# Softmax attentions: the values products of every step stand ahead of the step's other bank 7 work on TensorE

## Chip, cores and metric

The kernel is one program on one core of a Trainium2 chip. The metric is the device time of that core for one execution, in microseconds (us). Five engines work side by side, each through its own instructions in the order in which they are written: TensorE (PE; its weight loads are listed as PEld), ScalarE (ACT), VectorE (DVE), GpSimd (POOL) and SyncE (SP, here the issuer of most DMAs). They wait for one another by semaphores.

## What is computed

A chain of four layers, each an attention and a feed-forward part, each added to its input `x` after a layer norm. The rows are 4096 tokens of 128 features. Two of the attentions are softmax attentions with 16 heads of 8 features, and they alone are touched:

```python
# x: (16, 256, 128)
# L1_attn: causal, with biases
qkv = x @ Wqkv + bqkv
scores = einsum('bthd,bshd->bhts', q, k * D ** -0.5) + causal_mask
context = einsum('bhts,bshd->bthd', softmax(scores), v)
out = context.reshape(B, S, E) @ Wout + bout
# L3_attn, gated_attention: no mask, no bias
attn = softmax(einsum('bhqd,bhkd->bhqk', q, k) * HD ** -0.5)
out = moveaxis(einsum('bhqk,bhkd->bhqd', attn, v), 1, 2).reshape(b, l, d)
return out @ Wout * sigmoid(x @ Wgate)
```

The kernel takes both in 16 batches of 256 tokens.

## The kernel before, in words

Both softmax attentions are one function, `phase_attention`. The first one (causal, with biases) lies at about 192 to 516 us of the profiled execution, the second one (no mask, with a routing of tokens to experts behind it, `sort`) at about 1171 to 1461 us. Every engine runs through the same list `steps`: batches b from -2 to 16, and in each 8 steps s. A step handles two of a batch's 16 heads, and several batches are in flight.

What TensorE does in step (b, s) of `pe`, in its order:

- the **scores**, twice: `turned_scores(b, s)` with keys as rows (L1302, L1308 and, where causal, a mask at L1315), into banks 4 and 5, which ScalarE then turns into exponentials (`exponentials`, L1489, one ACTIVATE of 1024 columns in a step); and `scores(c, p)` of the next batch in natural order (L1333), into banks 0 to 3, of which VectorE takes the maxima (L1566). The turned scores of a step wait for the exponentials of the step before, since they reuse its two banks.
- the **values products** `values_of(b, s)` (L1353): four heads' exponentials times the values, 8 instructions in the trace, accumulated in bank 6. Steps 2 to 7 do groups 0, 1, 2 of batch b in two halves each, and steps 0 and 1 do group 3 of batch b - 1. The second half of group 3, in step 1, raises `pv_done` for the last time for batch b - 1. The first product of batch b, in step 2, overwrites bank 6 and waits for `o_kept(b - 1)`.
- **one piece of work that shares bank 7**, another in each step: step 0 turns the normalised rows of batch b - 2 (`ln.pe`, L268; for even b from 4 on in the second attention it first waits for `places`, which VectorE makes in step 7 of an odd batch, L2655 to L2662); step 1 projects queries and keys of batch b + 2 (`project_next`, L1207); step 2 turns the maxima (L1404) and multiplies with the router (L1426); step 3 turns the sums of batch b - 1 (`turn_values`, L1366); step 4 turns the divided heads (L1372); step 5 projects out (L1411); step 6 turns maxima (L1404, which waits for VectorE's reading of the projection, `proj_read`, L3151) and projects values (L1417); step 7 ranks the tokens in odd batches of the second attention (L2642 to L2647).

ScalarE's own order in step 1 is: exponentials, then `high(b + 2)` (L1216, two instructions that copy the projection out of bank 7 and wait for `qk_ready`, raised by L1207), then `keep_sums(b - 1)` (L1515, which copies bank 6 and raises `o_kept`). VectorE's order in step 3 is: maxima (L1566), then `normalised` (L1580, L1583), which waits for L1366. In step 4 of an odd batch it chooses experts, in step 5 it finishes batch b - 1 and takes statistics, and in step 7 it makes the places.

Of the kernel before, what the change touches and what calls it, by code (L numbers as in the profile page):

```python
# [1147 lines left out]
def phase_attention(k, name, w, biased, causal, finish, ln, front, sort=None, spares=None):  # L1148
# [22 lines left out]
    def has(c):  # L1171
        return 0 <= c < BATCH
# [9 lines left out]
    def nat_of(b, s):  # L1182
        return (b + 1, s - 1) if s else (b, 7)
# [99 lines left out]
    def pe(pe):  # L1283
# [3 lines left out]
        def turned_scores(b, s, turn):  # L1287

            g, x, half, par = s // 2, s % 2, s // 4, b % 2
            pair = (2 * x, 2 * x + 1)  # L1290
            if turn == 0:
                if s % 4 == 0:
                    pe.wait_ge(e["mt_kept"].sem, e["mt_kept"].at(b, half + 1))
                if s:
                    pe.wait_ge(e["prob_ready"].sem, e["prob_ready"].at(b, s))
                elif has(b - 1):
                    pe.wait_ge(e["prob_ready"].sem, e["prob_ready"].at(b - 1))
            if turn in (1, 2):
                kt = turn - 1
                for r in pair:  # L1300
                    t = slice(32 * r, 32 * r + 32)
                    pe.matmul(ps[:, 4 + r % 2, kt * 256:kt * 256 + 256], ka[t, par, g, kt * P:kt * P + P], qa[t, par, g, :],  # L1302
                              start=(kt == 0), stop=False, skip_group_check=True)
            if turn == 3:
                for kt in range(2):
                    for r in pair:
                        t = slice(32 * r, 32 * r + 32)
                        ins = pe.matmul(ps[:, 4 + r % 2, kt * 256:kt * 256 + 256], sel[t, g % 2, kt, :], mt[t, half, :],  # L1308
                                        start=False, stop=not causal, skip_group_check=True)
                if not causal:  # L1310
                    ins.then_inc(e["st_ready"].sem, 1)
            if turn == 4 and causal:
                for r in pair:
                    for kt in range(2):
                        ins = pe.matmul(ps[:, 4 + r % 2, kt * 384:kt * 384 + P], mnat[:, 0:P], i100,  # L1315
                                        start=False, stop=True, skip_group_check=True)
                ins.then_inc(e["st_ready"].sem, 1)

        def scores(c, p, turn):
            g, x, par = p // 2, p % 2, c % 2  # L1320
            if turn == 0:
                if p % 4 == 0:
                    sig = here(c, p // 4)
                    pe.wait_ge(sig.sem, sig.at(c // 2))
                if p >= 2:
                    pe.wait_ge(e["max_ready"].sem, e["max_ready"].at(c, p - 1))
                elif has(c - 1):
                    pe.wait_ge(e["max_ready"].sem, e["max_ready"].at(c - 1, p + 7))
            if turn in (1, 2):
                qt = turn - 1  # L1330
                for a in range(2):
                    t = slice(32 * (2 * x + a), 32 * (2 * x + a) + 32)
                    ins = pe.matmul(ps[:, 2 * x + a, qt * 256:qt * 256 + 256], qa[t, par, g, qt * P:qt * P + P], ka[t, par, g, :],  # L1333
                                    start=(qt == 0), stop=not causal, skip_group_check=True)
                if turn == 2 and not causal:
                    ins.then_inc(e["nat_ready"].sem, 1)
            if turn == 4 and causal:
                for a in range(2):
                    pe.matmul(ps[:, 2 * x + a, 0:P], i100, mnat[:, 0:P], start=False, stop=True, skip_group_check=True)
                    ins = pe.matmul(ps[:, 2 * x + a, 384:512], i100, mnat[:, 384:512], start=False, stop=True,  # L1340
                                    skip_group_check=True)
                ins.then_inc(e["nat_ready"].sem, 1)

        def values(c, g, kt):
            if kt == 0:
                pe.wait_ge(e["prob_ready"].sem, e["prob_ready"].at(c, 2 * g + 2))
                if g == 0:
                    pe.wait_ge(e["v_kept"].sem, e["v_kept"].at(c))
                    if has(c - 1):
                        pe.wait_ge(e["o_kept"].sem, e["o_kept"].at(c - 1))  # L1350
            at, col = at_window(g), 256 * (g % 2)
            for r in range(4):
                ins = pe.matmul(ps[32 * r:32 * r + 32, 6, col:col + 256], Vp[:, c % 2, 4 * kt + r, at:at + 32],  # L1353
                                PT[:, g % 2, r, kt * 256:kt * 256 + 256], start=(g == 0 and kt == 0),
                                stop=(g >= 2 and kt == 1), tile_position=(0, 32 * r), skip_group_check=True)
            if kt:
                ins.then_inc(e["pv_done"].sem, 1)
# [11 lines left out]
        def turn_heads(c):  # L1369
            pe.wait_ge(e["heads_ready"].sem, e["heads_ready"].at(c))  # L1370
            for t in range(2):
                ins = pe.transpose(ps[:, 7, t * P:(t + 1) * P], on[:, t, :], cst["ident"])  # L1372
            ins.then_inc(e["heads_turned"].sem, 1)

        def project_next(c):
            if has(c - 2):
                pe.wait_ge(e["mt_kept"].sem, e["mt_kept"].at(c - 2, 1))
            if has(c - 1):
                pe.wait_ge(e["qk_split"].sem, e["qk_split"].at(c - 1))
            if has(c - 2):  # L1380
                pe.wait_ge(e["v_kept"].sem, e["v_kept"].at(c - 2))
            if has(c - 4):
                pe.wait_ge(ln.e["xt_ready"].sem, ln.e["xt_ready"].at(c - 4))
            project(pe, c)
# [35 lines left out]
        def route(c):  # L1420
            pe.wait_ge(ln.e["xt_ready"].sem, ln.e["xt_ready"].at(c))
            if has(c - 1):
                pe.wait_ge(ln.e["logits_read"].sem, ln.e["logits_read"].at(c - 1))
            n = ln.router.shape[1]
            for j in range(2):
                ins = pe.matmul(ps[:, 7, 256 + j * n:256 + (j + 1) * n], ln.tail_t[:, j * P:(j + 1) * P], ln.router,  # L1426
                                start=True, stop=True)
            ins.then_inc(ln.e["logits_ready"].sem, 1)

        def values_of(b, s):  # L1430
            if has(b if s > 1 else b - 1):
                values(*((b, s // 2 - 1, s % 2) if s > 1 else (b - 1, 3, s)))

        for b, s in steps:
            c, p = nat_of(b, s)
            for turn in range(5):
                if has(b):
                    turned_scores(b, s, turn)
                if has(c):
                    scores(c, p, turn)  # L1440
            if s in (0, 2):
                values_of(b, s)
            if s == 1 and b >= 0 and has(b + 2):
                project_next(b + 2)
            if s == 2 and has(b):
                turn_maxima(b, 1)
            if s == 2 and has(b - 2):
                route(b - 2)
            if s == 3 and has(b - 1):
                turn_values(b - 1)  # L1450
            if s == 4 and has(b - 1):
                turn_heads(b - 1)
            if s == 5 and has(b - 1):
                project_out(b - 1)
            if s == 6 and has(b + 1):
                turn_maxima(b + 1, 0)
                project_values(b + 1)
            if s == 0 and has(b - 2):
                if has(b):
                    pe.wait_ge(e["v_kept"].sem, e["v_kept"].at(b))  # L1460
                if sort and b >= 4 and b % 2 == 0:
                    pe.wait_ge(sort.e["places"].sem, sort.e["places"].at(routed(b - 1)))
                ln.pe(pe, b - 2)
            if s == 7 and routed(b) is not None:
                if has(b + 1):
                    pe.wait_ge(e["mt_kept"].sem, e["mt_kept"].at(b + 1, 1))
                    pe.wait_ge(e["v_kept"].sem, e["v_kept"].at(b + 1))
                pe.wait_ge(e["proj_read"].sem, e["proj_read"].at(b - 1))
                pe.wait_ge(ln.e["logits_read"].sem, ln.e["logits_read"].at(b - 2))
                sort.rank(pe, routed(b), count)  # L1470
            if s not in (0, 2):
                values_of(b, s)
        if sort:
            pe.wait_ge(sort.e["places"].sem, sort.e["places"].at(NBLK - 2))
        ln.pe(pe, BATCH - 1)
# [1841 lines left out]
```

## Time and profile before

| | |
|---|---|
| median of three runs | 1843.84 us (1843.05 to 1846.98) |
| the profiled execution | 1847.87 us, its span 1846.0 us |
| mean granted clock of TensorE | 0.901 of 2.4 GHz |
| TensorE busy | 1516.4 us, 82% of the span |
| VectorE busy | 1150.8 us, 62% |
| ScalarE busy | 849.2 us, 46% |
| GpSimd busy | 568.4 us, 31% |

The span is what lies between the first and the last instruction of the trace. The rest of an execution's time, 1.9 us here, lies around it. Busy shares are averages over some ten phases with different limits, so for a change in one phase only that phase's stretch is of use. In the timelines "idle before" is time in which the engine did nothing, with the instruction that ended it.

### The profile page before, as it was taken

To read this page: it belongs to the slowest core of one execution; us is meant where nothing else is said; L and a number is where in the kernel's file an instruction comes from. 1 tells how busy PE (TensorE), PEld (TensorE's weight loads), DVE (VectorE), ACT (ScalarE), POOL (GpSimd) and SP (SyncE) were. 2 spreads that over 40 slices of the span, in tenths; PEclk is the share of its full clock that TensorE was granted. 3 is DMA by queue.
4 is the path that set the end of the run, shared out by engine and by line. 5 is a ranking of instruction groups with operands and counts; after the bars stand their busy time and mean duration, and the time that the engine had idled before them with its cause. 6 is when DMAs were issued, how large, how long until landed. Compare 5 with 4: busy or idle time off the path is not lost. (4 is left out here: it accounts for less than half of the span.)

```text
span 1846.0 us, 46915 instructions
## 1 busy us (share of the span) xinstructions
PE 1516.4 (82%) x16703; PEld 1119.7 (61%) x16703; DVE 1150.8 (62%) x3234; ACT 849.2 (46%) x1633; POOL 568.4 (31%) x780
## 2 busy tenths in 40 slices
PE   4979799999978997779998878699999499531993
PEld 3745566666545665658887555455555299521993
DVE  5855577777557765736564477788887454564344
ACT  2422356656511123533443335566665478301784
POOL 5111011111111111433320231113333546476565
PEclk9989799999989998999999898799998799755996
DMA  4000222222049900000000100223332044221334
GB/s 188 1 2 0 70 59 59 58 58 56 19 134 329 314 2 0 1 2 3 3 3 3 70 1 1 62 66 81 81 84 61 31 116 135 78 87 49 90 94 157
DMA packets 84685, 125.00 MB, mean 68 GB/s; under 512 B 17328, under 2 KB 70576, under 8 KB 82928
## 3 DMA queue, kind: packets, MB, share of 16 engines
q1 hardware_dynamic: 75824, 104.30, 19.2%
q0 software_dynamic: 8640, 17.78, 2.7%
q8 instruction: 136, 2.23, 0.5%
q14 instruction: 85, 0.70, 0.1%
HBM read 67.47 MB, written 55.59 MB: 67 GB/s over the span
## 5 line engine op out<-in xcount | busy, mean ns | idle before, releaser
L1566 DVE TENSOR_REDUCE small<-ps 128x8 f32<-128x1024 f32 (+1 forms) x256 | 311.5, 1223 | 93.3 <-PE ps L1340 67.5
L1489 ACT ACTIVATE scr<-ps 128x1024 f32<-128x1024 f32 x256 | 262.0, 1024 | 180.4 <-PE ps L1315 109.4
L248 POOL TENSOR_TENSOR rstd<-vare,neghalf 128x4 f32<-128x4 f32 (+1 forms) x72 | 63.2, 878 | 391.8 <-DVE vare L227 391.3
L1353 PE MATMUL ps<-scr 128*32 128x256 f32 x2048 | 165.8, 396 | 4.2 <-ACT scr L1515 3.5
L2907 POOL DMA_INDIRECT results<-scr x142 | 136.0, 958 | 95.2 <-DVE scr L2894 46.6
L2841 PE MATMUL ps<-scr 128*128 128x128 f32 x1136 | 153.6, 280 | 0.0
L1302 PE MATMUL ps<-scr_r 32*128 32x256 f32 x1024 | 131.5, 334 | 23.6 <-ACT scr L1489 14.6
L1302 PEld LDWEIGHTS ps<-scr_r 32*128 32x128 f32 x1024 | 79.0, 187 | 116.2 <-ACT scr L1489 57.8
L1333 PE MATMUL ps<-scr_r 32*128 32x256 f32 x1024 | 134.2, 343 | 10.6 <-DMA scr_r<-scr_r 6.1
L2841 PEld LDWEIGHTS ps<-scr 128*128 128x128 f32 x1136 | 142.2, 197 | 0.0
L2887 DVE TENSOR_TENSOR scr<-ps,scr 128x256 f32<-128x256 f32 x142 | 60.3, 425 | 123.8 <-ACT scr L2878 116.2
L1955 PEld LDWEIGHTS ps<-scr 64*64 64x64 f32 x4480 | 107.5, 135 | 39.7 <-ACT scr L2143 10.8
L1955 PE MATMUL ps<-scr 64*64 64x64 f32 x4480 | 119.8, 222 | 13.8 <-DVE scr L2245 7.0
L788 ACT ACTIVATE scr<-ps 128x512 f32<-128x512 f32 x72 | 43.0, 597 | 168.5 <-PE ps L718 168.5
L171 POOL TENSOR_TENSOR neghalf<-neghalf 128x1 f32<-128x1 f32 x80 | 15.8, 197 | 323.6 <-DVE small L1573 152.1
L1308 PE MATMUL ps<-scr_r 32*128 32x256 f32 x1024 | 104.8, 280 | 0.0
L1333 PEld LDWEIGHTS ps<-scr_r 32*128 32x128 f32 x1024 | 80.1, 194 | 13.8 <-issue 5.6
L742 PEld LDWEIGHTS ps<-region,scr 128*128 128x128 f32 x576 | 71.8, 191 | 26.6 <-DVE scr L855 16.9
L742 PE MATMUL ps<-region,scr 128*128 128x128 f32 x576 | 78.5, 279 | 6.8 <-DVE scr L855 6.8
L268 PE MATMUL ps<-w_const,xn 128*128 128x128 f32 x224 | 44.4, 324 | 46.2 <-DVE xn L235 19.4
L1308 PEld LDWEIGHTS ps<-scr_r 32*128 32x128 f32 x1024 | 81.8, 189 | 0.0
L2707 POOL DMA_INDIRECT rows_m<-XT,small x60 | 60.5, 1008 | 67.2 <-PE ps L1308 60.1
(415 smaller groups left out, 3503.5 us busy)
## 6 DMA issues: line engine op xcount, KB each, us to landing
scr_r<-scr_r SPq DMA_DIRECT2D x512, 64.0 KB
rows_m<-kinds SPq DMA_DIRECT2D x8, 2064.0 KB, 29.1
rows_f<-kinds SPq DMA_DIRECT2D x8, 2064.0 KB, 73.1
scr<-results SPq DMA_DIRECT2D x32, 256.0 KB
scr<-rows_m SPq DMA_DIRECT2D x71, 64.5 KB
scr<-rows_f SPq DMA_DIRECT2D x71, 64.5 KB
scr<-in_l3m SPq DMA_DIRECT2D x1, 3072.0 KB, 9.9
results<-scr POOLq DMA_INDIRECT x142
```

The lines of the kernel that those rows point to most:

```text
L248: pool.tensor_tensor(k.rstd[:, 0:self.J], k.vare[:, 0:self.J], k.neghalf[:, 0:self.J], ALU.pow).then_inc(self.e["rstd_ready"].sem, 1)
L742: ins = pe.matmul(ps[:, 4 + y % 2, j * P:(j + 1) * P], hT[:, c % 2, j * P:(j + 1) * P], down[:, c * P:(c + 1) * P], start=(c % per_y == 0 ...
L1302: pe.matmul(ps[:, 4 + r % 2, kt * 256:kt * 256 + 256], ka[t, par, g, kt * P:kt * P + P], qa[t, par, g, :], start=(kt == 0), stop=False, sk ...
L1308: ins = pe.matmul(ps[:, 4 + r % 2, kt * 256:kt * 256 + 256], sel[t, g % 2, kt, :], mt[t, half, :], start=False, stop=not causal, skip_grou ...
L1333: ins = pe.matmul(ps[:, 2 * x + a, qt * 256:qt * 256 + 256], qa[t, par, g, qt * P:qt * P + P], ka[t, par, g, :], start=(qt == 0), stop=not ...
L1353: ins = pe.matmul(ps[32 * r:32 * r + 32, 6, col:col + 256], Vp[:, c % 2, 4 * kt + r, at:at + 32], PT[:, g % 2, r, kt * 256:kt * 256 + 256] ...
L1489: act.activation(PT[:, g % 2, 2 * x:2 * x + 2, :], ps[:, 4:6, :], ACT.Exp).then_inc(e["prob_ready"].sem, 1)
L1566: dve.tensor_reduce(nf[:, half, 0:blocks, at:at + 2].rearrange("p q a -> p a q"), ps[:, 2 * (p % 2):2 * (p % 2) + 2, :].rearrange("p a (q ...
L1955: return pe.matmul(out, left, right, start=start, stop=stop, tile_position=pos, skip_group_check=True)
L2707: pool.indirect_dma_start(self.rows, bass.IndirectOffsetOnAxis(ap=self.place[:, n, t:t + 1], axis=0), self.kept[:, t, :], None).then_inc(s ...
L2841: ins = pe.matmul(hidden_at(j)[:, 256 * n + P * c:256 * n + P * c + P], here[:, j % DEEP, n, P * c:P * c + P], xT[:, j % DEEP, :], start=T ...
L2907: pool.indirect_dma_start(results, bass.IndirectOffsetOnAxis(ap=names[:, j % IN, P:P + 1], axis=0), y[:, j % OUT, :], None).then_inc(store ...
```

## The change

Of the values products, those of steps 0 and 2 stood ahead of the bank 7 work of their step, and those of the six other steps stood behind it. Now all eight stand ahead of it. Nothing is added or removed, no wait is changed, and the other engines' programs are as before.

```diff
                 if has(c):
                     scores(c, p, turn)
-            if s in (0, 2):
-                values_of(b, s)
+            values_of(b, s)
             if s == 1 and b >= 0 and has(b + 2):
                 project_next(b + 2)
...
                 sort.rank(pe, routed(b), count)
-            if s not in (0, 2):
-                values_of(b, s)
         if sort:
```

## Rows read from the trace of the kernel before

**Rows 1.** Stretches: length, busy PE PEld DVE ACT POOL (x instructions), PEclk, DMA share, GB/s.

```profile
212.00:500.00 288.00, 279.75 (x3828) 187.03 (x3828) 203.88 (x379) 172.67 (x269) 40.41 (x132) 1.00 0.21 53
...
1200.00:1415.00 215.00, 195.89 (x2490) 119.42 (x2492) 181.75 (x394) 147.15 (x233) 70.53 (x141) 1.00 0.30 78
```

**Rows 2.** TensorE's waits in the first attention: total us, times, longest.

```profile
PE ps L1302 <- issue: 5.9, 16, 0.4
```

**Rows 3.** TensorE's waits in the second attention, same columns.

```profile
PE ps L1302 <- ACT scr L1489: 11.1, 24, 1.5
...
PE ps L1353 <- ACT scr L1515: 3.5, 13, 0.3
...
PE ps L1404 <- issue: 3.4, 6, 0.6
```

**Rows 4.** Chain of work that ended last, second attention, batch 7: start, us, what.

```profile
1298.68 1.07 PE ps L1207 x4
...
1299.78 0.02 ACT scr_r L1216
...
1300.51 0.61 ACT scr L1515
...
1301.25 0.64 PE ps L1353 x8
...
1303.29 0.63 PE ps L1366 x4
...
1303.92 0.57 PE ps L1353 x8
```

**Rows 5.** Timeline, first attention: start, us, engine, line, tiles, count [idle before].

```profile
339.89 1.08 PE L1207 MATMUL ps<-XT,scr 128*128 128x256 f32 x4
...
341.01 0.84 ACT L1216 ACTIVATE scr_r<-ps,small 128x256 fp32r<-128x256 f32 x2
...
341.74 0.60 ACT L1515 ACTIVATE scr<-ps 128x512 f32<-128x512 f32 x1
...
342.70 0.64 PE L1353 MATMUL ps<-scr 128*32 128x256 f32 x8
```

**Rows 6.** Timeline, second attention, batch 7, steps 3 to 8.

```profile
1303.09 1.23 DVE L1566 TENSOR_REDUCE small<-ps 128x4 f32<-128x1024 f32 x1 [0.34 <-PE ps L1333]
...
1304.24 0.35 DVE L1580 RECIPROCAL scr<-ps 128x32 f32<-128x32 f32 x1
...
1308.97 0.41 DVE L3151 TENSOR_TENSOR scr<-ps,region 128x256 f32<-128x256 f32 x1
...
1314.38 0.18 DVE L2662 CAST small<-xn 128x8 int32<-128x8 f32 x1
...
1314.68 0.41 PE L268 MATMUL ps<-w_const,XT 128*128 128x128 f32 x2 [0.65 <-issue]
```

**Rows 7.** Timeline, second attention, batch 6, step 1.

```profile
1281.90 0.56 ACT L298 ACTIVATE scr<-ps,w_l3a 128x256 f32<-128x256 f32 x1 [0.59 <-PE ps L268]
...
1282.61 1.10 PE L1207 MATMUL ps<-XT,scr 128*128 128x256 f32 x4
```

**Rows 8.** Timeline, second attention, batch 6, step 7 into step 0 of batch 7.

```profile
1294.10 0.46 ACT L1507 ACTIVATE scr<-ps 128x128 f32<-128x128 f32 x2
...
1294.97 1.02 ACT L1489 ACTIVATE scr<-ps 128x1024 f32<-128x1024 f32 x1 [0.42 <-PE ps L1308]
...
1296.09 0.39 PE L1302 MATMUL ps<-scr_r 32*128 32x256 f32 x2 [0.60 <-ACT scr L1489]
```

**Rows 9.** Stretches around batch 14 of the second attention, columns of rows 1.

```profile
1413.00:1417.00 4.00, 2.82 (x44) 1.54 (x42) 3.40 (x7) 3.10 (x4) 0.87 (x4) 1.00 0.44 117
...
1417.00:1419.00 2.00, 2.00 (x20) 0.98 (x15) 1.23 (x1) 1.02 (x1) 1.02 (x1) 0.51 0.14 36
```

**Rows 10.** Timeline, second attention: step 1 of batch 14 and of batch 15.

```profile
1414.66 0.38 PE L1302 MATMUL ps<-scr_r 32*128 32x256 f32 x2
...
1435.43 0.50 PE L1302 MATMUL ps<-scr_r 32*128 32x256 f32 x4 [0.17 <-ACT scr L1489]
```

## The prediction

> **What bounds the kernel now.** The change touches two stretches only, so the averages of the page are of no use, and I read the stretches themselves. The windows view shows TensorE busy 97% of the middle of the first attention (279.75 of 288 us) and 91% of that of the second (195.89 of 215), with VectorE next at 71% and 85%, all at the full 2.4 GHz [rows 1]. So the first attention has hardly anything to give, and the second at most some 1.5 us in a batch.
>
> Then TensorE's waits. In the first attention there is one group that comes once in a batch: 0.37 us in front of the turned scores, 5.9 us over 16 [rows 2]. In the second there are three [rows 3]: the turned scores wait for exponentials (11.1 us), the first values product of a batch waits for ScalarE's copy of bank 6 (L1515; 3.5 us, 13 times 0.27), and the turn of the maxima in step 6 waits (3.4 us, 6 times 0.57) for VectorE's reading of the projection: L3151 begins at 1308.97 and takes 0.41 [rows 6]. The last is in odd batches only, where VectorE chooses experts in step 4.
>
> Last the chain of waits, batch 7, steps 1 and 2. It doesn't run along TensorE alone. It goes projection (L1207, from 1298.68), ScalarE's two copies of it (L1216, from 1299.78), ScalarE's copy of bank 6 (L1515, 1300.51 to 1301.11), and from there to the first product of batch 7 at 1301.25 [rows 4]. This is the path that the change meets. The copy of bank 6 needs nothing of the projection, but it stands behind L1216 in ScalarE's order.
>
> **Part by part.** Nothing is added or removed. No DMA is issued by the moved instructions, and no other queue's order changes. A block of products takes 0.57 us of TensorE's path (L1353 on the chain) [rows 4]. All exponentials that the products read have been waited for by the turned scores of the same step already, so no product gains a wait by its place. What moves is: the bank 7 work of steps 1 to 7 ends 0.57 us later within its step, and TensorE's sum stays the same.
>
> *Step 1.* `qk_ready` comes 0.57 later, hence L1216, hence L1515, since ScalarE works in order. That `pv_done` now comes 1.1 us sooner helps nobody: L1515 didn't wait for it. In the second attention the first product of the batch already waits 0.27 for L1515 [rows 3], so all of 0.57 is lost there. In the first attention L1207 began at 339.89, L1216 at 341.01, L1515 ran from 341.74 to 342.34, and the product started at 342.70 [rows 5]. By the second attention's 0.14 from the end of L1515 to the product [rows 4] it could have started at 342.48, so there is a cover of 0.22, and 0.57 - 0.22 = 0.35 is lost. VectorE's low parts and the next exponentials shift as well; both stay in front of what TensorE reaches at the new time (L1489 would end about 1302.6, the next turned scores come at 1303.1).
>
> This happens in every batch with a projection ahead and a copy behind, b = 1 to 13: 13 times. First attention: 13 x 0.35 = **+4.6 us**.
>
> *Second attention, b = 1 and 2*: 2 x 0.57 = +1.1. *Even b = 4 to 12*: here step 0 waits for the places, so the normalised rows are late; L298 runs from 1281.90 to 1282.46 and L1207 starts only at 1282.61 [rows 7]. `project_next` waits for it. Products in front cover that 0.15, which leaves 0.42: 5 x 0.42 = +2.1.
>
> *Odd b = 3 to 13*: the 0.57 goes to VectorE. From 1303.09, where its maxima begin at the scores' release, to 1314.68 it has no idle time: maxima, L1580, experts, L3151, norm, places (L2662, 1314.38 + 0.18), and then TensorE's L268, which waited 0.65 for them [rows 6]. So the step 0 wait sets the batch's end. In step 3 the turn of the sums (L1366, 0.63 from 1303.29 [rows 4]) goes behind 0.57 of products. By my estimate it waited some 0.1 for ScalarE's copy of the logits before and doesn't any more, so it ends about 0.5 later in its step, at 1304.4 on the old scale, and L1580, which began at 1304.24 [rows 6], begins 0.2 later. Together 0.57 + 0.21 = 0.78: 6 x 0.78 = +4.7. The 0.57 wait in step 6, the visible gain of the change, is filled by the products, but this pays nothing, because the places are later than TensorE anyway. Batch 15 has the 0.2 alone.
>
> *Step 6.* In even batches the values copy (L1507, from 1294.10, 0.46 long) ended 0.41 before the exponentials of step 7 began (1294.97), and these hold up the next scores (1296.09) [rows 8]. L1507 moves by 0.57, and it overlaps the next by about 0.1, so the exponentials come some 0.07 later: 7 x 0.07 = +0.5. Steps 4 and 5 cost nothing: the divided heads and the projection now have 0.57 more before they are wanted, and ScalarE's copies of them still end before the exponentials of their step are due.
>
> Sum: 4.6 + 1.1 + 2.1 + 4.7 + 0.2 + 0.5 = **+13.2 us**. The profiled execution of 1847.87 us (span 1846.0 and 1.9 around it) would become 1861.1. It lies 4.0 above the median of the three runs, 1843.84, and the same sum on that gives **1857.0 us**. Bounds for the late copy of bank 6, of which the sum holds 4.6 + 1.1 + 2.1 + 6 x 0.57 = 11.2 us: nothing, if it were hidden, and 0.57 in all 26 batches, 14.8. Below nothing is excluded for it, since the same three instructions run in the same order, only later.
>
> **Rivals.** *The delay is swallowed.* TensorE waits 11.1 us for exponentials in the second attention [rows 3]. If that slack took up the late product, the second attention would lose nothing and win the 6 x 0.57 of step 6, and with the first one's +4.6 the time would be 1845. Against it: exponentials wait for scores of their own step, so they move along with a late step and their distance stays.
>
> *The gain arrives and the loss doesn't* (the other side). Place: step 6 of the odd batches, price 6 x 0.57 = 3.4, so 1840.4. It decides if ScalarE's copies L1216 don't hold up L1515, that is if the product's wait is really on something else, and if the places come sooner with TensorE. For it: 0.27 is a small wait and could be a mere latency. Against: the chain passes through L1216 and L1515 in this order [rows 4], and VectorE is without a gap up to the places [rows 6].
>
> *The clock falls.* In 1413 to 1417 TensorE was busy 2.82 of 4 us, with two short waits, and then the granted clock was 0.51, that is 1.2 GHz [rows 9]. Step 1 of batch 14 to step 1 of batch 15 took 1435.43 - 1414.66 = 20.8 us [rows 10], where batch 6 to batch 7 took 1298.68 - 1282.61 = 16.1 [rows 4, 7]: 4.7 us for such a fall. The change puts a wait of 0.8 in step 2 a few us behind that for the places, which grows to 1.1, in each even batch, so TensorE's busy share around there comes close to the 70% at which it fell. One more fall gives 1862, all five 1880; the one that is there could also vanish, 1852. Against it: the mean clock from 1200 to 1415 is 1.00 [rows 1], with the same 0.65 wait for the places in batches 4 to 12.
>
> The Trainium skill, "TensorE: Matmul & The Clock Gate", section "A second HAM failure mode: psum-queue depth-cycling", says that frequent micro-idles between groups of matmuls can make the clock swing between its levels. This case's trace agrees as far as batch 14 goes [rows 9], where no single wait was over 0.7 us; by that rule this rival is the likely one.
>
> **How the numbers follow.** Forecast (13.2 us lost, the clock as before) 0.62; clock falls more often 0.19; delay swallowed 0.12; gain without loss 0.07. The likeliest gives 1857.0. The lower end has to let in the sum at half its size and the swallowed case, 1845; the upper one or two further falls, 1868; the rest of the clock case and the gain lie outside. What a measurement of this kernel can tell from no change is about 0.2%, or 3.7 us: faster is the gain (0.07), same the swallowed case (0.12), slower the other two (0.81).
>
> **What would show it.** After the change the first product of a batch waits about 0.85 for L1515 in the second attention 13 times, and there is a new group of waits of about 0.35 in the first. The 0.57 in front of L1404 shrinks to about 0.3, the wait in front of L268 grows to about 1.1, batches of the first attention take 0.35 more, pairs of batches of the second 1.3 more. The prediction is wrong if L1515 starts at the same distance from the projection as before yet the products don't wait, if the periods stay, or if PEclk shows more stretches at 1.2 GHz than before.

## The result: 28.9 us slower, twice what was forecast

Median 1872.33 us (1867.85 to 1877.58, 4 runs) against 1843.46 for the kernel before; the ratio is 1.015, with a 95% interval of 1.0132 to 1.0168. The forecast was 1857.0 with a range of 1845 to 1868. The profiled execution took 1877.58 us, span 1875.7, against 1847.87 and 1846.0; it is the slowest of the four, so the stages below add up to a little more than the 28.9 us of the medians.

Where the 29.7 us of span between the two profiled executions lie, from the start of the instruction that opens a stage to the start of the one that closes it:

| stage | before | after | difference |
|---|---|---|---|
| up to the first attention (first L1333) | 191.8 | 193.3 | +1.5 |
| first attention (to the last L1426) | 323.9 | 336.0 | +12.1 |
| its expert FFN (to the last L742) | 183.3 | 183.9 | +0.6 |
| delta rule and FFN (to the last L742) | 395.9 | 399.9 | +4.0 |
| inputs of the second attention | 76.0 | 76.0 | 0.0 |
| second attention (L1333 to L1426) | 289.3 | 300.4 | +11.1 |
| the rest | 385.8 | 386.2 | +0.4 |

The forecast had +4.6 for the first attention, +8.6 for the second and nothing elsewhere.

The middle of both attentions, columns of rows 1 (stretch, length, busy us of PE, PEld, DVE, ACT, POOL, then PEclk), of the kernel after:

```profile
213.00:511.00 298.00, 286.47 (x3800) 188.04 (x3799) 205.65 (x377) 172.49 (x267) 40.46 (x132) 1.00 0.20 51
1219.00:1435.00 216.00, 189.42 (x2415) 115.94 (x2407) 177.47 (x379) 142.69 (x227) 67.02 (x137) 1.00 0.28 75
```

TensorE's busy share went from 97% to 96% and from 91% to 88%. TensorE's waits in the first attention (line, what it waited for, total us, times, longest), and then in the second; ScalarE's copy of bank 6, L1515 before, is L1512 here:

```profile
PE ps L1302 <- issue: 5.9, 16, 0.4
...
PE ps L1353 <- ACT scr L1512: 3.8, 13, 0.3
```

```profile
PE ps L1302 <- ACT scr L1486: 11.9, 36, 0.6
PE ps L1353 <- ACT scr L1512: 10.9, 13, 0.8
...
PE ps L1404 <- issue: 1.4, 6, 0.3
```

These are the waits that the prediction named. A new group stands in the first attention, 13 times 0.29 us, and the one in the second has grown from 13 times 0.27 [rows 3] to 13 times 0.84. The 0.57 in front of L1404 [rows 3] has shrunk to 0.23.

The path in the second attention, batch 7, steps 1 and 2 (timeline of the kernel after):

```profile
1319.69 0.38 PE L1302 MATMUL ps<-scr_r 32*128 32x256 f32 x2 [0.17 <-ACT scr L1486]
...
1320.36 0.64 PE L1353 MATMUL ps<-scr 128*32 128x256 f32 x8
...
1320.92 1.13 PE L1207 MATMUL ps<-XT,scr 128*128 128x256 f32 x4
...
1322.09 0.84 ACT L1216 ACTIVATE scr_r<-ps,small 128x256 fp32r<-128x256 f32 x2 [0.60 <-PE ps L1207]
...
1322.82 0.60 ACT L1512 ACTIVATE scr<-ps 128x512 f32<-128x512 f32 x1
...
1323.56 0.64 PE L1353 MATMUL ps<-scr 128*32 128x256 f32 x8 [0.84 <-ACT scr L1512]
```

The products of step 1 stand at 1320.36, so the projection comes at 1320.92, 1.23 after the step's start instead of 0.67 (in batch 6 of the kernel before it was 0.82, 1282.61 [rows 7] less 1281.79). ScalarE waits 0.60 for it, and the copy of bank 6 and the next product follow at the old distances [rows 4]. From one step's scores to the next, this odd batch now goes, from step 1 on through step 7 to step 0 behind it, 2.29, 2.86, 1.90, 1.85, 1.88, 2.34, 2.03, 2.72 us, where it went 2.30, 2.29, 1.90, 1.85, 1.88, 2.67, 1.90, 2.28: the 0.57 is lost in step 2, 0.33 comes back in step 6, and 0.57 more is lost in steps 7 and 0 (0.13 and 0.44), in front of the places:

```profile
1336.92 0.18 DVE L2659 CAST small<-xn 128x8 int32<-128x8 f32 x1
...
1337.22 0.41 PE L268 MATMUL ps<-w_const,XT 128*128 128x128 f32 x2 [1.07 <-issue]
```

So in the second attention the sum holds: a pair of batches takes 34.47 us instead of 33.22, +1.25, where +1.27 was worked out. In the first attention it doesn't. There a batch takes 19.72 us instead of 18.77, +0.95 instead of +0.35, and only 0.29 of it is a wait. (Such a time, from a step to the same step of the next batch, is called the period below.)

### The profile page after: what moved, and what is told of

Same layout as the page of the kernel before. It is cut to its first block and busy times, and to the rows that moved or that the text cites. A ratio compares the mean times of both kernels' runs of the same rounds, so it can differ in the third digit from the quotient of the medians.

```text
span 1875.7 us, 46915 instructions
## 1 busy us (share of the span) xinstructions
PE 1532.2 (82%) x16703; PEld 1126.3 (60%) x16703; DVE 1154.6 (62%) x3234; ACT 849.8 (45%) x1633; POOL 568.2 (30%) x780
## 5 line engine op out<-in xcount | busy, mean ns | idle before, releaser
L1353 PE MATMUL ps<-scr 128*32 128x256 f32 x2048 | 167.4, 399 | 15.2 <-ACT scr L1512 14.7
L1333 PE MATMUL ps<-scr_r 32*128 32x256 f32 x1024 | 133.0, 341 | 10.5 <-DMA scr_r<-scr_r 6.0
L1952 PEld LDWEIGHTS ps<-scr 64*64 64x64 f32 x4480 | 108.8, 136 | 40.2 <-ACT scr L2140 11.1
L171 POOL TENSOR_TENSOR neghalf<-neghalf 128x1 f32<-128x1 f32 x80 | 15.8, 197 | 339.2 <-DVE small L1570 160.5
L742 PEld LDWEIGHTS ps<-region,scr 128*128 128x128 f32 x576 | 71.8, 191 | 26.8 <-DVE scr L855 17.1
L1333 PEld LDWEIGHTS ps<-scr_r 32*128 32x128 f32 x1024 | 79.4, 192 | 13.7 <-issue 5.6
L742 PE MATMUL ps<-region,scr 128*128 128x128 f32 x576 | 78.5, 279 | 7.1 <-DVE scr L855 7.1
```

The costliest lines, as they stand in the source:

```text
L742: ins = pe.matmul(ps[:, 4 + y % 2, j * P:(j + 1) * P], hT[:, c % 2, j * P:(j + 1) * P], down[:, c * P:(c + 1) * P], start=(c % per_y == 0 ...
L1952: return pe.matmul(out, left, right, start=start, stop=stop, tile_position=pos, skip_group_check=True)
```

## The experiments

The theories. **COPY** is the prediction's: products ahead in step 1 make ScalarE's copy of bank 6 late. **SWITCH** came from laying the first attention's steps side by side. In the kernel before, step 5, L1411 behind a mask matmul, and products behind one in step 7 (timeline; PEld rows are weight loads):

```profile
349.47 0.22 PE L1340 MATMUL ps<-w_mask 128*128 128x128 bf16 x1
...
349.47 0.53 PEld L1411 LDWEIGHTS ps<-scr 128*128 128x128 f32 x4
...
349.52 0.66 PE L1411 MATMUL ps<-scr 128*128 128x128 f32 x4
...
354.21 0.22 PE L1340 MATMUL ps<-w_mask 128*128 128x128 bf16 x1
...
354.36 0.16 PEld L1353 LDWEIGHTS ps<-scr 128*32 128x32 f32 x8
354.36 0.64 PE L1353 MATMUL ps<-scr 128*32 128x256 f32 x8
```

The last mask begins at 349.47 in the first case, and the bank 7 work begins 0.05 behind it. The products begin 0.15 behind theirs (354.21), and their first weight load doesn't begin any sooner. The rows differ in the form of the array: masks and bank 7 work use it as 128*128, products as 128*32, scores as 32*128. With products ahead, step 5 of the kernel after reads:

```profile
357.12 0.22 PE L1340 MATMUL ps<-w_mask 128*128 128x128 bf16 x1
...
357.27 0.64 PE L1353 MATMUL ps<-scr 128*32 128x256 f32 x8
...
357.84 0.71 PE L1411 MATMUL ps<-scr 128*128 128x128 f32 x4
358.48 0.18 PEld L1302 LDWEIGHTS ps<-scr_r 32*128 32x128 f32 x2
```

0.15 + 0.57 + 0.64 = 1.36 us from the last mask to the next scores, where it was 0.05 + 0.60 + 0.57 = 1.22. SWITCH says that a change of form costs about 0.1. Over the whole middle of the first attention (212 to 505 us, the medians of all such neighbours in the kernel before) it comes to 0.09 each time: a matmul that follows a mask starts 0.056 behind it in the same form and 0.149 in another, behind a 128x128 f32 matmul it is 0.110 and 0.203, behind one with 256 columns 0.216 and 0.309. The order scores, masks, bank 7, products, scores changes form three times, the order scores, masks, products, bank 7, scores four times. The second attention has no masks and changes three times in either order.

Laid side by side, from the start of the last mask to the start of the next scores (us, one batch of the first attention from 338.8 on in the kernel before and from 345.8 on in the kernel after):

| step | 1 | 2 | 3 | 4 | 5 | 6 | 7 | 0 |
|---|---|---|---|---|---|---|---|---|
| before | 1.64 | 1.44 | 1.16 | 1.11 | 1.22 | 1.39 | 1.16 | 1.11 |
| after | 1.78 | 1.81 | 1.31 | 1.11 | 1.36 | 1.53 | 1.16 | 1.11 |

Steps 1, 3, 5 and 6 lose 0.14 or 0.15 each, with TensorE never waiting, and step 2 loses 0.37, where the wait for the copy stands. Together that is 0.94 of the 0.95. Of the 0.14, 0.09 is the one change more; the rest lies inside the bank 7 work, whose first two matmuls start 0.21 apart behind products and 0.17 apart behind a mask (step 5). **CLOCK** is the prediction's third rival, now for the 9 us that neither of the two explains: 13 x 0.95 and 6.5 x 1.25 are 20.5 of the 28.9.

**Products ahead in step 1 alone.**

```diff
-            if s in (0, 2):
+            ahead = s in (0, 1, 2)
+            if ahead:
                 values_of(b, s)
...
-            if s not in (0, 2):
+            if not ahead:
                 values_of(b, s)
```

> Only step 1's products are moved ahead (steps 0, 1, 2 ahead, the rest behind as before). Theory COPY (the late copy of bank 6 holds up the first product of a batch): it shows here in full, 0.35 us a batch in the first attention and about 0.55 in the second, so 13 waits of TensorE on L1515 in each. Theory SWITCH (in the first attention products that directly follow the 128x128 mask matmuls start 0.10 us later than bank 7 work does, and what follows the bank 7 work starts 0.04 later than products would have): it adds 0.14 in this one step. Together the first attention's period goes from 18.77 to about 19.27, the second's pair of batches from 33.22 to about 34.2, total +13 us, about 1856.5. A rival by which every moved step costs alike (28.9 / 6) gives +5 us, 1848.

Measured: 1858.0 against 1844.16, ratio 1.0073 (1.0056 to 1.0090), +13.8 us. First attention's period 19.28, a pair of the second 17.64 + 16.59 = 34.23. The 13 waits for the copy are there in both (3.7 and 10.9 us). One of six moved blocks brings half of the loss. COPY and SWITCH together give the 0.51 of the first attention (0.37 + 0.14); the rival by which every step costs alike falls. The periods make 13.2 us of the 13.8, and the median of the runs' mean clocks is 0.905, where the kernel before had 0.904: here the clock costs hardly anything in the median, although the profile has two falls in the second attention.

**Products ahead in all steps but step 1** (`ahead = s != 1`).

> All products ahead but those of step 1. COPY then costs nothing: no wait of 0.3 or 0.8 for L1515 beyond the 0.27 that was there in the second attention. SWITCH costs 0.14 in steps 3, 5 and 6 of the first attention and nothing in steps 4 and 7 (in 4 TensorE had a wait of the same size before), so the period is about 19.2 and the first attention 6.9 us longer. In the second the odd batches' late reciprocal costs some 0.2 each, 1.5 us. Total +8, about 1852. If SWITCH is wrong and the first attention's loss was all due to the copy, the period is 18.77 and the total at most +2.

Measured: 1859.74, ratio 1.0080 (1.0061 to 1.0099), +15.6. The first attention's period is 19.22, with no wait for the copy, so 0.45 a batch is lost there with TensorE never waiting: SWITCH. A pair of the second is 17.45 + 16.00 = 33.45. The two halves add up to the whole change: 0.51 + 0.45 = 0.96 of 0.95, 1.01 + 0.23 = 1.24 of 1.25. But the time is 8 us more than the steps explain, and the median of the mean clocks is 0.898.

**The new order in the second attention alone** (`ahead = s in (0, 2) or not causal`).

> The new order in the second attention alone. It has no masks, so SWITCH costs it next to nothing, and my sum of before (+8.6 us) should hold there: pairs of batches of 34.5 us instead of 33.22, first attention's period 18.77. Total about +10, 1853.5. What the full change has beyond it and beyond the first attention's 13 x 0.95 would be the granted clock in other stages, which differs from execution to execution.

Measured: 1860.03, ratio 1.0078 (1.0053 to 1.0103), +15.9, by the single runs 1848.4 to 1862.5. Period of the first attention 18.78, pairs 34.47, as expected; the total is 6 us over, 8 us more than 6.5 pairs at 1.25 make. The run of 1848.4 had a mean clock of 0.909, the one of 1862.5 had 0.896.

**The full change with the copy of bank 6 ahead of the projection's copies.**

```diff
+            if s == 1 and has(b - 1):
+                keep_sums(b - 1)
             if s == 1 and b >= 0 and has(b + 2):
                 high(act, b + 2)
-            if s == 1 and has(b - 1):
-                keep_sums(b - 1)
```

> The full change, and ScalarE copies bank 6 (L1515) ahead of the projection (L1216) in step 1. COPY: the waits for L1515 are gone in both attentions, also the 0.27 that the second one had before. First attention: period about 19.35 (SWITCH alone is left), second: pairs of about 33.0. Total about +7, 1850. If the copy isn't what costs, the time stays at 1872.

Measured: 1872.93, ratio 1.0144 (1.0112 to 1.0176), as slow as the full change. The expectation was wrong, and TensorE's waits say why (first attention, then second):

```profile
PE ps L1404 <- issue: 2.7, 13, 0.2
```

```profile
PE ps L1404 <- issue: 11.1, 19, 0.8
```

In the second attention (six of the 19 are the old ones of step 6) its timeline reads:

```profile
1323.04 0.64 PE L1353 MATMUL ps<-scr 128*32 128x256 f32 x8
...
1323.45 0.88 DVE L1225 SCALAR_TENSOR_TENSOR scr_r<-ps,small,scr_r 128x256 fp32r<-128x256 f32 x2 [1.59 <-ACT scr_r L1216]
...
1324.42 0.41 PE L1404 MATMUL ps<-w_const,scr_r 128*128 128x128 f32 x2 [0.75 <-issue]
```

The waits of L1353 are gone, and the same 13 come back one block later in front of the turn of the maxima. L1404 waits for `qk_split`, VectorE's low parts of the same projection (L1225), because both use bank 7; L1225 ends at 1324.33, 0.09 before it. So two paths lead from the projection to step 2, of nearly the same length, and freeing one only uncovers the other. The period is 19.61 instead of 19.72, a pair of the second attention 34.23 instead of 34.47. COPY was right on where the wait shows and incomplete on what it hangs on: it is the late projection.

**Masks ahead of the maxima products**, once with the old order and once with the new.

```diff
-            if turn == 3:
+            if turn == 3 and causal:
+                for r in pair:
+                    for kt in range(2):
+                        pe.matmul(ps[:, 4 + r % 2, ...], mnat[:, 0:P], i100, start=False, stop=False, ...)
+            if turn == 4:
                 for kt in range(2):
...
-            if turn == 4 and causal:
+            if turn == 3 and causal:
                 for a in range(2):
                     pe.matmul(ps[:, 2 * x + a, 0:P], i100, mnat[:, 0:P], ...)
```

> The order of before, but in the causal attention the mask matmuls (bf16, 128x128 weights) stand ahead of the maxima products L1308 instead of behind them. A reference for the next run: products and bank 7 work now both directly follow L1308, as in the second attention, where both start 0.32 us behind its start. SWITCH: steps 0, 2 and 7, whose products followed masks, win 0.10 each, and going from masks to L1308 may cost something new, so a period of 18.5 to 18.9 in the first attention. The second is unchanged.

> The full change with the masks early. SWITCH: without a mask matmul directly ahead of the products, steps 1, 3, 5 and 6 lose 0.04 each instead of 0.14, so the first attention's period is only about 0.55 above that of the order of before with early masks (0.35 for the copy, 0.16 to 0.2 for what follows bank 7 work), where it was 0.95 with late masks. Rival, the products' place costs whatever stands ahead of them: 0.95 again. Total about 6 us below the full change.

Measured: old order 1906.16 (ratio 1.0321, 1.0278 to 1.0364), period 21.73; new order 1912.24 (1.0376, 1.0344 to 1.0409), period 21.90. Moving the masks made the attention three us a batch slower in itself, far outside what I expected. It puts two more changes of form in each step. A step without waits, step 6, takes 2.80 us instead of 2.46, the others 0.20 to 0.44 more. Two changes at 0.09 are only 0.19 of that 0.34; where the rest comes from isn't shown. The rows with the old order, where L1337 and L1338 are the masks, L1313 is the maxima product, L1351 the values products and L1402 the bank 7 work of step 6:

```profile
360.91 0.22 PE L1338 MATMUL ps<-w_mask 128*128 128x128 bf16 x1
...
361.06 0.50 PE L1313 MATMUL ps<-scr_r 32*128 32x256 f32 x4
...
361.49 0.42 PE L1351 MATMUL ps<-scr 128*32 128x256 f32 x4
```

```profile
379.99 0.50 PE L1313 MATMUL ps<-scr_r 32*128 32x256 f32 x4
...
380.42 0.44 PE L1402 MATMUL ps<-w_const,scr_r 128*128 128x128 f32 x2
```

Behind L1313, products and bank 7 work both start 0.43 later, and the two orders differ by 0.17 a batch instead of 0.95. Step by step, from L1313 to the next scores, seven of the eight steps are the same in both orders within 0.01 us (2.06, 1.67, 1.62, 1.64, 1.81, 1.66, 1.62), also steps 1, 3, 5 and 6, which lost 0.14 each before. SWITCH holds: without equal forms to lose, the order costs nothing. What is left is all in step 2, 1.88 instead of 1.72, where the products start 0.58 behind L1313 with the new order:

```profile
364.72 0.50 PE L1313 MATMUL ps<-scr_r 32*128 32x256 f32 x4
...
365.30 0.42 PE L1351 MATMUL ps<-scr 128*32 128x256 f32 x4
```

That is COPY: TensorE idles 0.09 in front of them, too little for the view of the waits to list, and the longer steps cover the rest of the late copy. So of the 0.78 that vanished some 0.56 was SWITCH and 0.2 is covered COPY.

**Products ahead in steps 3 to 7 of the second attention alone** (`ahead = s in (0, 2) or (s != 1 and not causal)`).

> Products ahead in steps 3 to 7 of the second attention only; the first attention and step 1 as before. The steps' times say 0.23 us a pair of batches (33.45 against 33.22), 1.5 us in all. If the granted clock depends on the order in the second attention (theory CLOCK: more and longer waits around the places bring more stretches at 1.2 GHz), it is 6 to 10 us instead, with a mean clock a few thousandths lower than in the runs of before beside it. If the clock is only chance, the mean clocks are alike and the time is about 1845.5.

Measured: 1856.73 (9 runs) against 1847.28 (14 runs), ratio 1.0053 (1.0031 to 1.0075), +9.4 where the steps give 1.5. The medians of the runs' mean clocks are 0.896 and 0.902. That is what CLOCK said: about 8 us more than the steps hold, with a lower clock. The profile is of the fastest of the nine runs, so the 8 us themselves are in no trace. It does show falls inside the attention, here two of three (columns as above):

```profile
1249.00:1253.00 4.00, 3.92 (x32) 2.10 (x30) 2.55 (x4) 2.66 (x5) 0.88 (x4) 0.58 0.23 55
...
1285.00:1289.00 4.00, 3.85 (x34) 1.75 (x33) 2.04 (x4) 2.81 (x5) 1.25 (x4) 0.72 0.17 43
```

All fourteen profiles can be asked for this. From step 1 of batch 1 to step 1 of batch 13 of the second attention the granted clock never falls in the six profiles in which that attention has the old order. It falls once to three times in seven of the eight in which some or all of its products moved; only the profile of the kernel after has none. A fall inside cost 1.2 to 3.1 us, by the periods around it. The kernel with the new order in the second attention alone shows what came ahead of one:

```profile
1251.70 0.41 PE L268 MATMUL ps<-w_const,XT 128*128 128x128 f32 x2 [1.08 <-issue]
1253.76 2.08 PE L1207 MATMUL ps<-XT,scr 128*128 128x256 f32 x4
```

```profile
1249.00:1252.00 3.00, 1.65 (x25) 0.92 (x22) 2.42 (x8) 1.12 (x2) 0.00 (x0) 1.00 0.38 98
1252.00:1254.00 2.00, 2.00 (x23) 0.98 (x22) 1.96 (x2) 1.59 (x2) 0.43 (x2) 0.65 0.47 116
```

TensorE was busy 1.65 of 3 us, with the 1.08 wait for the places, and then fell to 1.2 GHz: the projection takes 2.08 us instead of 1.13. It is the place that the prediction named, though not in the way that it gave: the products ahead in steps 3 to 7 bring these falls with the wait of step 2 at its old 0.27, and the wait for the places, grown from 0.64 to 1.08, is enough. The same 1.07 or 1.08 stands at all six of these places in the kernel after, and there the clock fell behind none of them. In the kernel with step 1 alone the wait for the places stayed at 0.64, and its two falls come behind the 0.84 wait of step 2.

**The new order in the first attention alone** (`ahead = s in (0, 2) or causal`).

> The new order in the causal attention alone. Its period 19.72, the stretch 12.1 us longer, the second attention in pairs of 33.22. TensorE is without waits in the first attention, so CLOCK has nothing to say here: +12 us, 1856, with the mean clock as in the runs of before. If the clock suffers here as well, +16 or more.

Measured: 1863.12, ratio 1.0091 (1.0069 to 1.0113), +15.8. The attention took 336.2 us, +12.3, as expected, and the median of the mean clocks is 0.901, beside 0.902. The other 3.5 are in the delta stage (delta rule and FFN in the table of stages): it took 399.3 instead of 395.9, though nothing of it was changed.

**The delta stage.** In five profiles, all with a first attention 11 us longer or more, it took 399.3 to 400.2; in the five others 395.4 to 396.0. The last four kernels ask whether it is the order of the first attention (ORDER) or the time at which the stage begins (PHASE). VectorE writes a scratch tile at the end of the first attention, 25, 40 or 55 times:

```diff
+        if causal:
+            for _ in range(25):
+                dve.drain()
+                dve.memset(tmp, 0.0)
```

> The kernel before, with VectorE writing a scratch tile 25 times at the end of the first attention, so that everything behind starts some 6 us later. The stage of the gated delta rule and its FFN took 395.4 to 396.0 us in the profiles whose first attention was as before or up to 6.6 us longer, and 399.3 to 400.2 in the five profiles where it was 11 us longer or more, with a longer stretch at 1.2 GHz. Theory PHASE: it depends on when the stage begins, so with 6 us here about 395.7. Rival ORDER: only the changed order of the attention makes it 399, also 395.7 here.

> As before with 40 such writes, about 12 us later, like the first attention of the full change. PHASE: the delta stage takes 399 to 400 us, and the total is the delay and 4 us more. ORDER: it takes 395.7, and the total is the delay alone.

> As before with 55 writes, about 18 us later. PHASE: the length is one of the two, 395.7 or 399.5, depending on how the clock's changes fall. ORDER: 395.7.

> The full change with 25 writes behind the first attention. PHASE: the delta stage's length may be either 395.7 or 399.5. ORDER: it stays at 399 to 400. The first attention's steps are those of the full change, period 19.72.

Measured: each has one profile, and only the kernel with 40 writes has more runs. The stage begins (the start of the FFN's last instruction ahead of it) and takes, in us:

| kernel | delay by the writes | the stage begins | it takes |
|---|---|---|---|
| before | none | 699.0 | 395.9 |
| before, 25 writes | 9.0 | 708.4 | 400.0 |
| before, 40 writes | 13.8 | 713.9 | 398.9 |
| before, 55 writes | 20.3 | 718.8 | 395.2 |
| after | none | 713.2 | 399.9 |
| after, 25 writes | 8.1 | 718.9 | 400.7 |

ORDER falls: with the old order too, with nothing changed but writes ahead of it, the stage takes 400.0 and 398.9. PHASE fits the ten profiles that were there before (five that begin by 704.8 are short; of the five from 710.9 on all are long), but not as it was put: with 55 writes, and after the change with 25, the stage begins within 0.1 us of the same time and takes 395.2 and 400.7. So the time since the start of the execution doesn't settle the length, and with one profile of each kernel it isn't known how often the same kernel would give the other length. The total doesn't bear out the 4 us either: the kernel with 40 writes took 1862.6, ratio 1.0101 (1.0064 to 1.0137), 15.2 us more than the kernel before for a delay of 13.8. What the trace shows is where the 4 to 5 us are: in the granted clock. The same 12 us of the stage, 33 us behind its last L1678, for the kernel before, the one with 25 writes and the one with 55:

```profile
790.80:802.80 12.00, 8.06 (x116) 4.74 (x116) 5.40 (x9) 1.57 (x3) 4.23 (x4) 0.86 0.00 0
```

```profile
800.60:812.60 12.00, 8.90 (x83) 5.60 (x84) 4.64 (x7) 1.36 (x3) 3.03 (x3) 0.59 0.00 0
```

```profile
810.50:822.50 12.00, 8.04 (x116) 4.72 (x116) 5.40 (x9) 1.57 (x3) 4.25 (x4) 0.86 0.00 0
```

The granted clock is 0.59 in place of 0.86, and 83 instead of 116 matmuls are done in that time. The kernel after has 0.58 there. Over the whole stage 54.6 to 61.4 us are at 1.2 GHz in the six short profiles and 64.9 to 71.7 in the eight long ones.

## Why the prediction was wrong

The time came out 15.7 us above the forecast. The first attention's steps are 7.5 of it, the second attention's steps took 0.8 less than forecast (7.8 for 8.6), and the 9 that are left go with a lower clock in the second attention and in the delta stage.

*What bounds the kernel, the chain.* Right. The path through the projection, L1216 and L1515 to the first product is where the loss shows, 13 times in each attention.

*Step 1.* Right in size: 0.57 lost in the second attention (0.27 to 0.84), and 0.37 for 0.35 in step 2 of the first, of which 0.29 is listed as a wait. That the low parts on VectorE stay in front of what TensorE reaches was right for this kernel, but only by some 0.1, as the run with the copy first showed.

*Second attention, odd and even batches.* The pair came to +1.25 for +1.27; from step 1 to step 1 the odd batch lost 0.80 for 0.78 (the sums of the two rows of steps above) and the even one the remaining 0.45 for 0.49. The 0.07 of step 6 in it didn't come: steps 6 and 7 of the even batches stayed at 2.05 and 1.90. From L1207 in step 1 of batch 0 to that of batch 13 it is 222.42 instead of 214.60 us. The gain of step 6 was paid and lost again at the places, as worked out.

*"TensorE's sum stays the same."* This is the step that failed. In the first attention each moved block of steps 1, 3, 5 and 6 costs 0.14 more, since products come between two pieces of work of the same 128*128 form. In step 4 the bank 7 work had started 0.13 behind the mask instead of 0.05, which hides it. That is 4 x 0.14 = 0.56 a batch, with the 0.37 of step 2 about the 0.95 measured, and 12.1 - 4.6 = 7.5 of the 15.7 us missing in the median. The trace of before held it: in the timeline from which [rows 5] come, L1207 starts 0.05 behind the last mask (339.84) and the products 0.15 behind theirs (342.55). The Trainium skill, "TensorEngine Tiling (Array Packing)", section "Key Properties", says that changing the tiling mode drains the engine, as opposed to changing the tile within a mode. The trace agrees, with 0.09 us for each change of form, behind a mask matmul as behind bank 7 work. It was the rule that spoke against this change, and I didn't weigh it.

*The third rival.* The clock did fall more often inside the second attention, in seven of eight profiles with a changed order and in none of six without, and I had it as a rival with 0.19 instead of a term, although the prediction itself called it the likely one by the rule that it quoted. Its price of 4.7 us was read from the fall of batch 14, 13.7 us long; those inside cost 1.2 to 3.1. In the second attention, six profiles with the old order have 283.8 to 289.3 us from its first to its last instruction, mean 286.7; four with the new order have 293.2 to 305.3, mean 301.1. The difference of 14.4 is 8 by the steps, and the 6 that are left go with the clock. In the profile of the kernel after itself this share was small: the fall of batch 14 [rows 10] came in the last two batches instead, and the clock stayed down to the end of the stage, 3.3 us (11.1 less 7.8). With the delta stage's 4 that is 7.3, and the steps are 19.9 (12.1 and 7.8); the other 2.5 of the 29.7 lie in stages that nothing changed. That stage's part was not in the prediction in any form: a delay upstream was priced at its own length. The medians tell where the clock's share comes from. Writes and early masks aside, the median of the mean clocks is 0.896 to 0.900 in the five kernels with products moved in steps 3 to 7 of the second attention, and 0.901 to 0.905 in the kernel before, with step 1 alone and with the first attention alone. One of the prediction's own signs of being wrong, more stretches at 1.2 GHz, is there in the profile too: 389 us of the span in place of 364.

*The rivals of the other side.* Neither the swallowed delay nor the gain without loss happened. Exponentials moved with their scores, as argued.

What stays open: why the clock falls at one repetition of the same waits and not at the next, what decides between the two lengths of the delta stage, and so how large the clock's share would be on average. Ten or more profiles of one kernel would be needed. None of these versions beats the kernel before.

## What to carry to other kernels

Before a block of matmuls is moved, write down the array form of each neighbour (the `128*32` and `32*128` of the rows) and count the changes of form in either order; here one more of them in each of four steps, with no instruction added, cost 0.56 us a batch, more than the late copy did in that attention. A wait that is freed by moving independent work forward is worth only what the next release allows: two paths from one projection reached the same step within 0.1 us of one another (periods 19.72 and 19.61), and in the second attention the places ended every second batch whatever TensorE did. And when a change lengthens or shifts a stage, ask for the granted clock of all stages behind it before explaining the difference by the change itself.

## What the runs showed of the hardware

- A change of array form out of 128*128 costs TensorE 0.09 us in this kernel: from start to start 0.056 and 0.149 behind a bf16 mask matmul, 0.110 and 0.203 behind a 128x128 f32 one, 0.216 and 0.309 behind one with 256 columns. Behind a mask the next weight load begins 0.002 after the mask's start in the same form and 0.147 after it in another.
- With as many changes of form in either order (the two kernels with early masks), the place of the products costs nothing: seven of eight steps are the same within 0.01 us.
- The same stage, with the same instructions, took 395.2 to 396.0 or 398.9 to 400.7 us, by its time at 1.2 GHz; a delay of 9.0 or 13.8 us ahead of it went with the long one, and at a start within 0.1 us of the same time both lengths occurred.
- TensorE's clock fell to 1.2 GHz behind a stretch in which it was busy 1.65 of 3 us with no single wait over 1.1 us; at other repetitions of the same waits it stayed at 2.4 GHz.
